# One-hots ahead of the masks, both halves of a state together, and half of the later tiles turned by DMA transposes

## What is computed

```python
xn  = layernorm(x)
out = x + attention(xn) + moe(xn)
# attention, 16 heads of 16: heads 0..3 local softmax attention (window 128 and the one before, causal),
# heads 4..15 causal linear attention in blocks of 64 tokens:
#   q = softmax(q); k = elu(k) + 1
#   ctx[u] = cumsum over blocks of k^T v;  den[u] = cumsum of sum(k);  out[block u] = q @ (ctx/den)[u-1]
# then @ Wo + bo
# moe: scores = xn @ router_w.T, top 2 of 8 experts, softmax of the two scores,
#   sum of w_e * (gelu(xn @ w1[e].T) @ w2[e].T), 1024 hidden
```

## Time and profile before

| | |
|---|---|
| time, median of 3 runs | 806.2 us (802.04, 806.2, 806.52) |
| profiled execution | 804.93 us, its span 803.2 us |
| busy PE / DVE / ACT / POOL | 706.1 / 459.0 / 405.9 / 429.5 us |
| mean granted PE clock | 0.946 of full |

### The profile page before, as it was taken

One profiled execution on the slowest core, in us unless ns is written; L12 is line 12 of the kernel. 1 busy time (PEld: TensorE's weight loads), 2 busy tenths in 40 slices (PEclk: granted clock), 3 DMA queues, 4 the chain that ended last, 5 costly groups with the idle time before them and its releaser, 6 DMA issues.

```text
span 803.2 us, 21487 instructions
## 1 busy us (share of the span) xinstructions
PE 706.1 (88%) x6866; PEld 555.4 (69%) x6867; DVE 459.0 (57%) x1540; ACT 405.9 (51%) x1115; POOL 429.5 (53%) x423
## 2 busy tenths in 40 slices
PE   1899999975887878898689999999999999999883
PEld 1666666743554545566478888888888888888662
DVE  6788887779978887865533333433444333334331
ACT  4788888733554545676344333444443444334331
POOL 6777777635444444477224555555655554543522
PEclk9999999969889887999699999999999999999998
DMA  8354333221131212132124444444444444433421
GB/s 255 119 158 134 120 107 107 93 66 47 49 84 51 70 43 72 46 114 57 50 53 67 78 77 75 77 79 78 77 77 74 77 79 73 72 64 57 61 44 20
DMA packets 87991, 64.26 MB, mean 80 GB/s; under 512 B 54675, under 2 KB 81556, under 8 KB 87924
## 3 DMA queue, kind: packets, MB, share of 16 engines
q1 hardware_dynamic: 73204, 43.69, 20.0%
q0 software_dynamic: 13632, 18.91, 15.5%
q10 hardware_dynamic: 1088, 0.79, 0.3%
HBM read 36.08 MB, written 17.96 MB: 67 GB/s over the span
## 4 chain that ended last, share of the span: by engine, by line
SPq 38%; PE 27%; DVE 15%; issue 9%; DMA 4%; ACT 4%; POOL 2%; DVEq 0%; POOLq 0%
SPq L688 37%; PE bank L279 9%; DVE ss L1303 4%; PE bank L1107 3%; DVE spare L505 3%; PE bank L1125 2%; PE bank L1066 2%; PE bank L1177 2%; DMA out<-attn,rows_to 2%; ACT ss L951 2%; PE bank L1128 1%; DMA out<-res,rows_to 1%; DVE xin L506 1%; PE bank L1086 1%; PE bank L1131 1%
## 5 line engine op out<-in xcount | busy, mean ns | idle before, releaser
L279 PE MATMUL bank<-stage,w1h 128*128 128x256 f16 (+1 forms) x1248 | 198.7, 267 | 6.1 <-DMA stage<-xin 4.7
L279 PE MATMUL bank<-stage,w1l 128*128 128x256 f16 (+1 forms) x624 | 164.9, 266 | 0.0
L1215 PE MATMUL bank<-w2h,pt 128*128 x568 | 154.9, 273 | 5.3 <-issue 4.0
L1215 PE MATMUL bank<-w2l,pt 128*128 x568 | 154.8, 273 | 0.0
L1215 PE MATMUL bank<-w2h,spare 128*128 x568 | 154.8, 273 | 0.0
L279 PEld LDWEIGHTS bank<-stage,w1h 128*128 x1248 | 115.9, 99 | 25.9 <-issue 8.9
L1026 ACT ACTIVATE pt<-ss 128x512 f16<-128x512 f32 (+1 forms) x78 | 41.9, 585 | 164.6 <-PE bank L1215 141.7
L876 POOL DMA_INDIRECT out<-res,rows_to x36 | 63.7, 1770 | 73.8 <-DMA stage<-rows 53.1
L876 POOL DMA_INDIRECT out<-attn,rows_to x35 | 61.9, 1769 | 73.4 <-DMA out<-attn,rows_to 47.7
L1477 DVE TENSOR_SCALAR res<-bank,tables 128x256 f32<-128x256 f32 x36 | 17.4, 484 | 96.3 <-PE bank L1215 78.6
L951 ACT ACTIVATE ss<-ss,negmax 128x256 f32<-128x256 f32 x128 | 63.8, 500 | 16.1 <-DVE negmax L1303 15.8
(11 more groups left out here) (242 smaller groups left out, 1661.8 us busy)
## 6 DMA issues: line engine op xcount, KB each, us to landing
stage<-w1c SPq DMA_DIRECT2D x16, 512.0 KB, 3.4
stage<-w2c SPq DMA_DIRECT2D x16, 512.0 KB
w1h<-x SPq DMA_DIRECT2D x16, 256.0 KB, 3.8
xn_rows<-w2h SPq DMA_DIRECT2D x32, 128.0 KB, 2.8
xb<-x SPq DMA_DIRECT2D x32, 128.0 KB, 2.8
out<-res SPq DMA_DIRECT2D x32, 128.0 KB, 2.0
stage<-xin SPq DMA_TRANSPOSE x144
stage<-rows SPq DMA_TRANSPOSE x140
```

The costliest lines, as they stand in the source:

```text
L279: ins = pe.matmul(dst, lhs(a, k), rhs(c, k), start=(n == 0), stop=(n == len(terms) - 1))
L1215: ins = pe.matmul(bY[h][:, 0:D], (hh, hl)[a][:, f, h * P:(h + 1) * P], (w2h, w2l)[c][:, DS(which * (FC * D) + f * D, D)], start=(f == a == ...
```

## The change

1. One-hots. On DVE, the first three columns of a batch are written right behind lrow, ahead of the wait for `pr_ps`; the other three right ahead of the masks. The table's products and sums come one step earlier (from step 18; TABLE = 28).
2. States. PE makes both halves' products of t-1 in one place, behind the transposes of q, into banks 5 and 2 (so nothing waits between them); the transposes of q go to bank 5. DVE adds both, one behind the other, late in the step (`state1_in`, `state2_in`); the addition behind lrow is gone. The value projection waits for `state2_in` in place of `qgt_in`. raw has four slots in place of two; krelu, state and qgt one buffer in place of two, with waits to suit.
3. Turning. Of the tiles from the ninth on (t >= 8) every odd one (9, 11, ... 31: twelve) is turned by four DMA transposes that SP issues behind `store_rows` in its step (2 to 13); PE's turning and ACT's copy of it are gone. Who reads such a tile waits for its DMAs.

```diff
-        state = pair("state", [P, 2, CTX])
-        raw = pair("raw", [P, 2, CTX])
+        state = 2 * [sb("state", [P, 2, CTX])]
+        raw = pair("raw", [P, 4, CTX])
...
+        def by_dma(t):
+
+            return t >= 2 * AHEAD and t % 2 == 1
...
+        def wait_turned(eng, t):
+
+            if by_dma(t):
+                eng.wait_ge(row_turned[t // 2 % 4], 64 * ((t // 2 - AHEAD) // 4 + 1))
+            else:
+                eng.wait_ge(s["xt_in"], nth(t))
...
+                def turn_row(u):
+                    if u // 2 - AHEAD >= 4:
+                        wait_turned(sp, u - 8)
+                    for k in range(2 * KC):
+                        sp.dma_start(turned_x(u)[:, k * P:(k + 1) * P], split_rows(u)[:, k * P:(k + 1) * P],
+                                     transpose=True).then_inc(row_turned[u // 2 % 4], 16)
...
                     if t.early(2):
                         store_rows(t.early(2)[0] // 2)
+                        turn_row(t.early(2)[1])
...
-                        if half_ == 0 and t.early(2):
-                            copy_turned(t.early(2)[1], b_xnt)
...
                 def router_of(t):
-                    pe.wait_ge(s["xt_in"], t + 1)
+                    wait_turned(pe, t)
...
-                    if HOT + 1 < t.t <= TABLE:
-                        route_table(pe, t.t - HOT - 2)
+                    if HOT < t.t <= TABLE:
+                        route_table(pe, t.t - HOT - 1)
...
-                    if t.early(2):
-                        pe.wait_ge(s["rl_in"], t.early(2)[1] + 1)
-                        pe.wait_ge(s["xt_in"], t.early(2)[0] + 1)
-                        turn_x(t.early(2)[1], b_xnt)
...
-                        add_to_state(t, 0)
+                        v = val[b][t.odd(-1)]
+                        parts = [(slice(0, 64), b_ctx[:, D:D + CTX]), (slice(64, P), b_tok1[:, D:D + CTX])]
+                        for r, dst in parts:
+                            pe.matmul(dst[:, 0:CB], ke[b][r, 0:GA], v[r, VL:VL + CB], start=True, stop=True)
+                        for r, dst in parts:
+                            ins = pe.matmul(dst[:, CB:CTX], ke[b][r, GA:2 * GA], v[r, VL + CB:VC],
+                                            start=True, stop=True)
+                        ins.then_inc(s["ctx_ps"], 1)
...
-                    if t.has(-1) and t.has(1):
-                        t.wait(s["state1_in"], -1)
-                        add_to_state(t, 1)
...
                         t.wait(s["v_in"], -1)
-                        t.wait(s["qgt_in"], -1)
+                        t.wait(s["state2_in"], -1)
...
-                            dve.tensor_tensor(raw[b][:, 0, :], b_state[:, b * CTX:(b + 1) * CTX], raw[b][:, 1, :], ALU.add)\
-                               .then_inc(s["state0_in"], 1)
+                    if HOT <= t.t < HOT + BATCHES:
+                        route_onehots(dve, t.t - HOT, 0, 3)
...
                     if HOT <= t.t < HOT + BATCHES:
-                        route_onehots(dve, t.t - HOT, 0, 3)
+                        route_onehots(dve, t.t - HOT, 3, CH)
...
+                        dve.tensor_tensor(raw[b][:, n + 1, :], b_ctx[:, D:D + CTX], raw[b][:, n, :], ALU.add)\
                            .then_inc(s["state1_in"], 1)
                         t.wait(s["state1_in"], -1)
-                        dve.reciprocal(rden[b][:].rearrange("p g u -> p u g"), raw[b][:, :, 0:CTX:CTX - 1])\
+                        t.wait(s["mask_in"], -3)
+                        dve.tensor_tensor(raw[b][:, (n + 2) % 4, :], b_tok1[:, D:D + CTX], raw[b][:, n + 1, :], ALU.add)\
+                           .then_inc(s["state2_in"], 1)
```

More of the change, by code:

```diff
@@ L176, in block_kernel @@
         rows_stored = [sem(f"rows_stored{n}") for n in range(SLOTS)]
-        raw_zero = sem("raw_zero")
+        raw_zero, begun = sem("raw_zero"), sem("begun")
         res_stored = [sem(f"res_stored{b}") for b in range(2)]
         xb_loaded = [sem(f"xb_loaded{b}") for b in range(2)]
+        row_turned = [sem(f"row_turned{n}") for n in range(4)]
         w_loaded = [sem(f"w_loaded{b}") for b in range(2)]
@@ L205, in scaled_x, with nth @@
             return x_pre[:, t % (2 * SLOTS), :]
+        def by_dma(t):
+            return t >= 2 * AHEAD and t % 2 == 1
+        def nth(t):
+            return sum(1 for u in range(t + 1) if by_dma(u) == by_dma(t))
+        def wait_turned(eng, t):
[3 more added lines that the diff above has]
+                eng.wait_ge(s["xt_in"], nth(t))
         def place(t):
@@ L831, in step @@
                         t.wait(s["state1_in"], -1)
-                        t.wait(s["lin_ps"], -3)
-                        pool.tensor_tensor(state[b][:], raw[b][:], ctx_mask[:].unsqueeze(1).to_broadcast([P, 2, CTX]),
+                        t.wait(s["lin_ps"], -2)
+                        n = 2 * t.odd(-1)
+                        pool.tensor_tensor(state[b][:], raw[b][:, n:n + 2, :], ctx_mask[:].unsqueeze(1).to_broadcast([P, 2, CTX]),
                                            ALU.mult).then_inc(s["mask_in"], 1)
@@ L1069, in scores_of @@
                                     ins.then_inc(s[f"head{h}"], 1)
-                def add_to_state(t, u):
-                    b, v, r = t.row(-1), val[t.row(-1)][t.odd(-1)], slice(u * 64, u * 64 + 64)
-                    dst = b_state[:, b * CTX:(b + 1) * CTX]
-                    pe.matmul(dst[:, 0:CB], ke[b][r, 0:GA], v[r, VL:VL + CB], start=True, stop=True)
-                    pe.matmul(dst[:, CB:CTX], ke[b][r, GA:2 * GA], v[r, VL + CB:VC], start=True, stop=True)\
-                        .then_inc(s[f"ctx{u}_ps"], 1)
                 def step(t):
@@ L1149, in step @@
                         t.wait(s["state1_in"], -2)
-                        if t.has(0):
-                            t.wait(s["state0_in"], 0)
-                        add_to_state(t, 0)
+                        t.wait(s["state2_in"], -2)
+                        v = val[b][t.odd(-1)]
[6 more added lines that the diff above has]
+                        ins.then_inc(s["ctx_ps"], 1)
                     if t.has(0):
@@ L1286, in _ @@
                         dve.memset(val[b][odd][:, VC - 1:VC], 1.0)
+                dve.wait_ge(raw_zero, 2)
+                for b in range(2):
+                    dve.memset(raw[b][:, 0, 0:CTX:CTX - 1], 1e-6).then_inc(begun, 1)
                 dve.wait_ge(pool_const, CONSTANTS)
```

49 lines of the change are left out of this document (23 added, 26 removed).

## The result

| | before | after |
|---|---|---|
| median | 805.0 us (802.04 to 806.52, 4 runs) | **782.8 us** (781.31 to 787.29, 4 runs) |
| after / before | | **0.974**, 95% interval 0.969 to 0.979 |
| profiled execution, span | 804.93, 803.2 us | 782.03, 780.3 us |
| busy PE / DVE / ACT / POOL | 706.1 / 459.0 / 405.9 / 429.5 | 679.3 / 441.8 / 400.6 / 418.9 us |
| mean granted PE clock | 0.946 | 0.953 |

The forecast was 790 us, the range 774 to 806. The change is worth 22 us where 15 were forecast. From the last result of attention, which SP stores at 372.51 us (before: 395.31), to the end both take 408 us (803.2 - 395.31, 780.3 - 372.51). So everything happens before it.

A forecast was written before the change was run, and what follows sets the result against it. PE was taken to bound steps 3 to 13; in steps 17 to 26 PE waited behind one-hots held up by POOL. 804.93 - 34 (one-hots, states) + 19 (DMA turning) = 790 us, range 774 to 806.

The forecast's parts named there:

- The sum: Whole kernel: 34 us less from one-hots and states, 19 more from DMA turning, 15 less in all.
- Steps with one-hots at 9.9 us, 34 less: Steps 17 to 26: from 13.3 to 9.9 us each, 34 us less over ten; bounds 28 and 48 less.
- PE's wait for qgt goes twice over: Steps 17 to 26: DVE reaches qgt some 3.2 us sooner, and the value projection waits for the second state instead.
- If none does, 8.5: Steps 17 to 26: if no POOL instruction holds DVE for its whole length, a step takes 8.5 us, 48 less.
- The upper bound: Steps 17 to 26: POOL's three instructions each hold DVE in full, 2.4 us lost, 10.5 us a step, 28 less.
- In the other steps the states change nothing: Steps without one-hots: same products, additions and masks; at worst 8 us over 20 steps, taken as nothing.
- Part 3, loop through SP of 11.3 us: Steps 3 to 13: store to transposes 2.2, issue 4.95, landing 2.3, result 1.6, clock 0.25; 11.3 us a step.
- Part 3 costs 19 us: DMA turning: 16 us more in steps 3 to 13, about 2 in step 2 and 1 in step 3; bounds 8 and 31.
- PE's saving: Steps 3 to 13: PE's dropped transposes, worth up to 8 us if the loop were under 9.1 us; not summed.
- Rival A: Steps 3 to 13: DMA turning is hidden, the loop stays under PE's step; 763 us, chance 0.10.
- rival B: Steps 3 to 13: transposes back up in SP's queue at 2.36 us each, loop 15.8 us; 840 us, chance 0.07.
- C: Within one per cent: POOL holds DVE in both places, 10.5 us a step, and the loop is 12.0; 804 us, chance 0.20.

The follow-up runs named there:

- e3: The kernel before with the first part alone: all six one-hots ahead of the masks, states and turning as before; 778.0 us, ratio 0.965.
- e5: The kernel before with the second part alone: states joined, one-hots in their old places, turning on PE; 788.8 us, ratio 0.977.
- e8: e1 with POOL waiting in steps 17 to 27 for the step's six one-hots before it adds the bias and scales; 751.8 us, ratio 0.932.
- e1: The changed kernel with its third part undone: PE turns and ACT copies the odd tiles again; 765.1 us, ratio 0.950.
- e2: The kernel before with the third part alone: DMA turning, one-hots and states as before; 814.0 us, ratio 1.010.
- e6: e1 with a state's two products apart: the first ahead of the transposes of q, the second behind them; 772.6 us, ratio 0.958.
- e4: The changed kernel with SP issuing the four transposes first in its step, ahead of the wait for the result; 764.5 us, ratio 0.950.
- e9: The changed kernel with the odd tile's router one step later on PE, SP's order unchanged; 766.5 us, ratio 0.953.
- e10: e9 with e8's wait on POOL and DVE's copy of the probabilities on ACT from the first step on; 750.9 us, ratio 0.934.
- e7: e1 with POOL's addition of the bias cut to one column of 256 in steps 17 to 27, a probe only; 755.1 us, ratio 0.937.
- e11: e1 with e8's wait on POOL and DVE's copy of the probabilities on ACT from the first step on; 748.9 us, ratio 0.931.

## Why the prediction was right

The time lay in the range and the sign was right. Of its steps:

- **The sum.** Forecast were 15 us less, measured 22.8 (profiled executions, to the last result of attention). Of the difference of 7.8 us, 9.7 come from the loop through SP, which was shorter than forecast, and 1.3 from steps 28 to 32; against it stand 2.7 us in steps 14 to 16 and about half a us in steps 17 to 27. (The lower end of the range, given as 776, comes to 775 from its own terms.)
- **Steps with one-hots at 9.9 us, 34 less: right within 4 us** (10.26 in the mean, 30.4 less; step 17 alone, at 12.65, is 2.7 of it). Another 3.05 us fell in step 27, for which nothing was forecast; a part of it is the shift of one-hots against the cuts, and came up again in step 16 (below). The reasons hold in part. "PE's wait for qgt goes twice over" was half wrong: moving the one-hots takes it away (e3), joining the states alone only moves it to the linear attention (e5). And the collisions with POOL were larger than in "a little": three pairs take 3.2 us for 1.1. "If none does, 8.5" is borne out by e8's 8.60. The upper bound counted 2.4 us lost; 2.1 were lost behind lrow, and none ahead of the masks.
- **"In the other steps the states change nothing [...] I take nothing": wrong, and the step that failed.** The term is -0.67 us a step, 7.4 in eleven (9.84 to 9.17, e1 and e5, with or without the new one-hots). In the kernel as changed it can't be seen, since the loop bounds those steps: it showed when the loop was gone, and it is why part 3 costs twice what e2 alone says. I had counted products and not asked on which side of a wait they stand. PE's timeline of before in step 7 had it:

```profile
87.07 0.49 PE L1074 MATMUL bank<-val,ke 64*128 64x129 f32 x2
...
89.95 0.49 PE L1074 MATMUL bank<-val,ke 64*128 64x129 f32 x2
...
90.53 0.66 PE L1177 MATMUL bank<-ident,ss 128*128 128x128 f32 x4
```

The second product (89.95) stood behind the wait for ACT's copy that ended at 89.17; moved ahead of it, it fills time in which the copy is made. e6 shows that this alone is enough for the early steps.
- **Part 3, loop through SP of 11.3 us: right mechanism, the landing too large.** e4 and e9 cut the loop at its two ends and each wins back all of it. Measured over ten steps: store to transposes 2.2 (2.2 forecast), four transposes 5.2 (4.95), landing and result 3.0, the slow clock included (3.9, and 0.25 for the clock). The landing was mis-sized: 2.3 from a gather that waited for eight transposes and from a batch at the end of the kernel, 1.2 in step 5. The step is 10.50, so the stretch grew by 7.3 us and not by 17.
- **Part 3 costs 19 us: nearly right as a price (17.7 by e1), for a reason that partly cancels.** The loop has its own length, whatever the rest of the step needs. Against the old step of 9.84 it costs 8.5 us in all (e2), against the 9.17 that the states make possible twice that. I held a loop that was too long against a step that was too long.
- **PE's saving isn't in the sum: right, and more than that.** With the loop cut (e4, e9) it would have been "worth up to 8 us"; it was worth nothing that can be measured against e1. PE then waits 0.8 us a step for DVE's qgt; but with 0.67 us of DVE's work gone (e10) the step fell by 0.1 only, so why nothing is gained stays open.
- **Rival A** (763 us, hidden) is near the time of e4 (764.5), in which the transposes are issued first, but by luck: its 8 us were PE's saved transposes, and what e4 gains in the early steps, e1 gains without them. In the kernel as changed, the order on SP decides. The transposes did not back up (rival B: one of 2343 ns, median 1233), and C's 10.5 us a step was not reached. B put the rows' stores of 2.52 us down to a queue full behind the weights' 512 KB; no row shows that, since the weights are issued 1.4 us ahead of the result's store in steps 9 and 10 alike, and the rows' stores take 0.90 us in the one and 2.52 in the other.
- **Steps 14 to 16: +2.7 us, not forecast.** Step 16 took 14.25 us before, at a granted clock of 0.91, and 17.23 in after:

```profile
194.20:211.43 17.23, 11.94 (x97) 7.83 (x93) 13.03 (x44) 6.96 (x23) 8.59 (x9) 0.70 0.15 47
```

Part of this is the shift against the cuts: this window now has the first three pairs of step 17 (44 instructions of DVE where there were 38). The two kernels without the move take 16.18 (e2) and 16.11 us (e5) here; after, e1, e3, e4 and e9 take 17.2 to 17.3, e6 takes 18.09, and the four with less of POOL beside the one-hots (e7, e8, e10, e11) 15.8 to 16.7. So about 1.1 us go with the three pairs. The other 1.9 are there with the third part alone and with the second alone, at granted clocks of 0.61 and 0.71 for the 0.91 of before; what in before keeps the step short is open and was not tried. The 1.95 us up to step 3 fit the forecast of 2 by luck: that start is 47.74 us in e1, which has no transposes, and 45.26 in e9, which has them.

## What to carry to other kernels

When work is moved to a queue that issues once a step, follow the whole circle: what the queue waits for, its issue time, the landing, who reads the data, and whether that reader stands ahead of what the queue waits for. If it closes, its length is a floor for the step that hardly shrinks when the rest of the step gets shorter (10.73 us in e2, 10.50 in after); issue ahead of the wait, or read a step later, and it is gone.

Price a moved instruction by the side of the next wait on which it lands, not by its count. And a relieved engine is worth something only if nothing else is just behind it: here PE lost four transposes a step for nothing, and DVE one copy for next to nothing.

Where DVE writes float16 from SBUF, look at what POOL runs beside it. A wait on POOL that keeps the two apart was the cheapest gain of this study, 13 us.

## What the runs showed of the hardware that was not expected

- Two groups of float32 matmuls on rows 0 to 63 and 64 to 127, into two banks and issued in turn, take the time of one: 0.60 us for both, 0.59 for each when they are apart (e1, e6). By the Trainium skill, "TensorEngine Tiling (Array Packing)", section "Key Properties", tiles of the array work independently and can run matmuls in parallel, and its "Gotcha 1: PSUM Pressure" wants different banks for different row tiles. The traces agree with the first; no run here tried one bank for both. Here it saved PE 0.6 us a step, and nothing of the early steps' time.
- What POOL costs DVE is told by the instructions that meet, not by the length of POOL's: 0.55 us less of POOL gave 1.0 us a step (e7), and keeping two instructions of 1.8 us together out of the place gave 1.4 (e8). By the Trainium skill, "SBUF — State Buffer", section "SBUF: two separate sides", POOL and DVE share a pair of ports that the first to start holds for its whole instruction; on DVE's side only some forms of instruction take it. The trace agrees for the float16 one-hots (0.24 and 0.29 us alone, 0.59 to 1.16 beside POOL). One of them gets through for each instruction of POOL, so a row of them is slowed to POOL's pace and not stopped. The float32 masks, which read a PSUM bank, aren't slowed (0.41 us).
- A DMA transpose of 128 x 128 float16 takes 1.23 us of SP's queue, and the data is there 2.4 us (median) behind its issue's start, 1.2 behind its end. Four cost 5 us of SP's queue here, while the DMA engines are busy for 0.44 of that stretch.
